# Expert weights held on chip and copied at a register's column, and spikes counted by TensorE, in a four-layer macaron kernel

## What is computed

```python
# L1 ffn: a spiking layer
h = relu(layernorm(x) @ W_fc.T) ** 2 @ W_proj.T      # 128 -> 512 -> 128
# 5 steps of a leaky integrate-and-fire neuron on input h:
#   mem = beta * mem + h - spike_before ; spike = mem > 1
# result: mean of the 5 spikes;  x = x + 0.5 * result
...
# L3 ffn, second half: a mixture of experts
ffn_probs = softmax(mean(n2, axis=1) @ ffn_rw + ffn_rb)     # one row for each sequence
topk_p, topk_i = top_k(ffn_probs, 2)
topk_p = topk_p / sum(topk_p)
h  = gelu(einsum('btd,bkdf->bktf', n2, fw1[topk_i]))        # 128 -> 256
eo = einsum('bktf,bkfd->bktd', h, fw2[topk_i])              # 256 -> 128
x  = x + einsum('bktd,bk->btd', eo, topk_p)
```

## Time and profile before

| | |
|---|---|
| median of 3 runs | 2145.94 us (2144.8 to 2148.79) |
| the profiled execution | 2153.13 us; its span, first to last instruction, 2151.4 us |
| the two spiking stages | from about 999 to 1054 us and 1224 to 1279 us of the span |
| the two expert stages | from about 1708 to 1763 us and 2083 to 2146 us |
| busy share of the span | TensorE 80%, VectorE 60%, ScalarE 54%, GpSimd 28% |

### The profile page before, as it was taken

How to read it: one execution, slowest core, us unless ns; L and a number is a source line. 1 busy time by engine, 2 the same in 40 slices (tenths; PEclk the granted TensorE clock), 3 DMA queues, 4 the chain that set the end, 5 groups by cost and what they waited for, 6 DMA issues and landing times.

```text
span 2151.4 us, 36562 instructions
## 1 busy us (share of the span) xinstructions
PE 1720.4 (80%) x13656; PEld 904.2 (42%) x13656; DVE 1294.6 (60%) x2595; ACT 1156.7 (54%) x2714; POOL 609.8 (28%) x759
## 2 busy tenths in 40 slices
PE   5896889788898879879468864986999777799976
PEld 1554345533355425543234322333555352355435
DVE  4773477444676357734667276835878445577844
ACT  3664356434465436554336545562888726388862
POOL 2551055200453025410155202303332020333202
PEclk8998999999899899989768687995999978599997
DMA  4000000000000000000063000005444020544403
GB/s 170 16 17 6 0 16 16 12 0 1 16 12 16 1 11 16 12 6 0 8 117 65 2 0 1 0 0 100 95 95 88 2 78 0 109 96 93 80 2 98
DMA packets 55270, 79.19 MB, mean 37 GB/s; under 512 B 6004, under 2 KB 38996, under 8 KB 54584
## 3 DMA queue, kind: packets, MB, share of 16 engines
q1 hardware_dynamic: 52536, 68.47, 14.5%
q0 software_dynamic: 2560, 8.39, 1.4%
HBM read 50.59 MB, written 16.88 MB: 31 GB/s over the span
## 4 chain that ended last, share of the span: by engine, by line
PE 55%; DVE 17%; ACT 14%; issue 7%; POOL 3%; DMA 3%; SPq 0%; DVEq 0%; POOLq 0%; ACTq 0%
PE ps L195 51%; ACT arena L544 4%; ACT arena L1208 2%; DVE arena L1229 2%; PE ps L463 2%; DVE arena L600 2%; ACT arena L267 2%; ACT arena L269 2%; DVE arena L643 1%; DVE arena L985 1%; DVE arena L987 1%; ACT arena L263 1%; DVE arena L983 1%; DMA arena<-scratch 1%; DVE arena L612 1%
## 5 line engine op out<-in xcount | busy, mean ns | idle before, releaser
L195 PE MATMUL ps<-arena 32*64 32x128 f32 (+10 forms) x10192 | 724.0, 319 | 129.9 <-ACT arena L1208 28.1
L195 PEld LDWEIGHTS ps<-arena 128*18 128x18 f32 (+6 forms) x10192 | 412.3, 128 | 434.8 <-issue 120.7
L1229 DVE TENSOR_REDUCE arena<-ps 128x2 f32<-128x512 f32 x512 | 322.4, 684 | 111.1 <-PE ps L195 109.1
L195 PE MATMUL ps<-arena,w_L0f 128*128 128x512 f32 (+3 forms) x800 | 352.1, 573 | 39.5 <-ACT arena L291 14.5
L1208 ACT ACTIVATE arena<-ps 128x512 f32<-128x512 f32 (+1 forms) x640 | 333.8, 576 | 78.7 <-PE ps L195 69.5
L544 ACT ACTIVATE arena<-ps,arena 128x128 f32<-128x128 f32 x512 | 226.2, 461 | 137.8 <-DVE arena L645 137.8
L195 PEld LDWEIGHTS ps<-arena,w_L0f 128*128 128x128 f32 (+2 forms) x800 | 149.4, 204 | 174.4 <-issue 127.0
L195 PE MATMUL ps<-arena,const 128*128 128x512 f32 (+1 forms) x528 | 173.1, 618 | 60.7 <-DVE arena L1657 22.3
L715 POOL TENSOR_TENSOR arena<-arena 128x512 f32<-128x512 f32 x128 | 132.2, 1040 | 239.6 <-DVE arena L617 239.6
L600 DVE TENSOR_TENSOR arena<-ps,arena 128x1024 f32<-128x1024 f32 x128 | 153.3, 1206 | 21.1 <-PE ps L195 21.1
L555 ACT ACTIVATE arena<-ps 128x512 f32<-128x512 f32 x128 | 76.8, 600 | 126.1 <-DVE arena L600 123.4
(11 more groups left out here) (223 smaller groups left out, 2150.0 us busy)
## 6 DMA issues: line engine op xcount, KB each, us to landing
scratch<-arena SPq DMA_DIRECT2D x40, 384.0 KB, 2.8
arena<-scratch SPq DMA_DIRECT2D x80, 192.0 KB
arena<-scratch SPq DMA_DIRECT2D x80, 128.0 KB
arena<-arena SPq DMA_DIRECT2D x64, 128.0 KB, 2.3
arena<-scratch SPq DMA_DIRECT2D x80, 88.0 KB
w_L0f<-in_L0f SPq DMA_DIRECT2D x2, 1557.0 KB, 12.3
arena<-arena SPq DMA_DIRECT2D x80, 12.0 KB
const<-in_const SPq DMA_DIRECT2D x1, 1276.0 KB, 7.6
```

The lines of the kernel that those rows point to most:

```text
L195: return self.nc.tensor.matmul(o, lhsT, rhs, start=start, stop=stop, skip_group_check=True)
L1229: o = V.tensor_reduce(mx, ps[:, self.score_bank(s), :].rearrange("p (t s) -> p t s", t=2), AXX, ALU.max)
```

## The change

Spiking stage. The spike of each step is written by itself, as a bf16 tile `fired[i]` of ones and zeros, with a compare of one source (lines 996, 1003); `mem` is then the plain sum of that tile and `u` (1001). `acc` is gone: TensorE adds the five tiles of a chunk, each multiplied by the bf16 unit matrix `ident_b`, in PSUM bank 6 or 7 (`count`), and VectorE adds the count to the residual (`add`, line 1014), one chunk late. There are ten `fired` tiles, for two chunks. TensorE's `count(c - 2)` stands between the up and the down products of chunk c.

Expert stage. SP loads all eight experts (8 DMAs of 256 KB) into `experts` at the stage's start. The 16 indirect DMAs are gone, and GpSimd has no work in the stage. VectorE turns each pair's expert number into a first column; for each pair it loads that number into a register (`value_load`), and copies 512 columns of `experts`, from the column in the register on, to `chosen[n]`. The first three copies are made ahead of the loop, then one in each turn, three pairs ahead. TensorE waits for `picked` in place of the DMA.

```diff
@@ Spike.tensor
             for j in range(4):
                 self.wait_ge(eng, self.relued, 4 * c + j - 3)
                 mm(ps[:, j, :], k.wp("L1f", "fcT")[:, j * P:(j + 1) * P], self.h[:, chunk(c)]).then_inc(self.up.sem, 1)
+            if c >= 2:
+                self.count(eng, c - 2)
...
+        self.count(eng, NCHUNK - 2)
+        self.count(eng, NCHUNK - 1)
+    def count(self, eng, c):
+        k = self.k
+        self.norm.wait_done(eng, 3)
+        self.wait_ge(eng, self.added, c - 1)
+        for i in range(SPIKE_STEPS):
+            self.wait_ge(eng, self.spiked, SPIKE_STEPS * c + i + 1)
+            k.mm(k.ps[:, 6 + c % 2, :], k.ident_b[:], self.fired[SPIKE_STEPS * (c % 2) + i], start=i == 0, stop=i == SPIKE_STEPS - 1).then_inc(self.counted.sem, 1)
@@ Spike.vector
-            ch.did(V.tensor_scalar(mem, y, -1.0, None, ALU.mult))
-            ch.wait_ge()
-            V.tensor_scalar(acc, mem, -1.0, None, ALU.is_lt)
-            for _ in range(SPIKE_STEPS - 1):
-                ch.did(V.scalar_tensor_tensor(u, mem, BETA, y, ALU.mult, ALU.subtract))
+            fired = self.fired[SPIKE_STEPS * (c % 2):SPIKE_STEPS * (c % 2 + 1)]
+            self.wait_ge(eng, self.counted, SPIKE_STEPS * (c - 1))
+            V.tensor_scalar(fired[0], y, 1.0, None, ALU.is_gt).then_inc(self.spiked.sem, 1)
+            ch.did(V.scalar_tensor_tensor(u, y, -BETA, y, ALU.mult, ALU.subtract))
+            for i in range(1, SPIKE_STEPS):
                 ch.wait_ge()
-                ch.did(V.scalar_tensor_tensor(mem, mem, -1.0, u, ALU.is_lt, ALU.add))
+                self.wait_ge(eng, self.spiked, SPIKE_STEPS * c + i)
+                ch.did(V.tensor_tensor(mem, fired[i - 1], u, ALU.add))
                 ch.wait_ge()
-                ch.did(V.scalar_tensor_tensor(acc, mem, -1.0, acc, ALU.is_lt, ALU.add))
-            ch.wait_ge()
-            V.scalar_tensor_tensor(k.X[:, cs], acc, 0.5 / SPIKE_STEPS, k.X[:, cs], ALU.mult, ALU.add)
+                V.tensor_scalar(fired[i], mem, -1.0, None, ALU.is_lt).then_inc(self.spiked.sem, 1)
+                if i < SPIKE_STEPS - 1:
+                    ch.did(V.scalar_tensor_tensor(u, mem, BETA, y, ALU.mult, ALU.subtract))
+            if c:
+                self.add(eng, c - 1)
+        self.add(eng, NCHUNK - 1)
+    def add(self, eng, c):
+        k, X = self.k, self.k.X[:, chunk(c)]
+        self.wait_ge(eng, self.counted, SPIKE_STEPS * (c + 1))
+        k.nc.vector.scalar_tensor_tensor(X, k.ps[:, 6 + c % 2, :], 0.5 / SPIKE_STEPS, X, ALU.mult, ALU.add).then_inc(self.added.sem, 1)
@@ L3Experts
-                eng.wait_ge(self.arrived[n].sem, self.arrived[n].at(16))
+                self.wait_ge(eng, self.picked, n + 1)
...
-        ch.did(V.tensor_scalar(self.rowf, self.rowf, k.C("partition"), None, ALU.add))
+        ch.did(V.tensor_scalar(self.rowf, self.rowf, float(EXPERT_N // P), None, ALU.mult))
         ch.wait_ge()
         V.tensor_copy(self.row_no, self.rowf).then_inc(self.rows_ready.sem, 1)
+        self.wait_ge(eng, self.arrived, 16 * EXPERTS)
+        self.wait_ge(eng, self.rows_ready, 1)
+        for n in range(AHEAD):
+            self.pick_expert(eng, n)
         for n in range(N + 2):
+            if n + AHEAD < N:
+                self.pick_expert(eng, n + AHEAD)
...
-    def gpsimd(self, eng, ch):
...
-            eng.indirect_dma_start(self.chosen[n], None, self.k.ins["experts"], bass.IndirectOffsetOnAxis(ap=rows, axis=0)).then_inc(self.arrived[n].sem, 16)
+    def pick_expert(self, eng, n):
+        i = n % TOP_K * BATCH + n // TOP_K
+        at = eng.value_load(self.row_no[0:1, i:i + 1], min_val=0, max_val=(EXPERTS - 1) * EXPERT_N)
+        self.k.nc.vector.tensor_copy(self.chosen[n], self.experts[:, bass.ds(at, EXPERT_N)]).then_inc(self.picked.sem, 1)
+    def sync(self, eng):
+        for e in range(EXPERTS):
+            eng.dma_start(self.experts[:, e * EXPERT_N:(e + 1) * EXPERT_N], self.k.ins["experts"][e * P:(e + 1) * P]).then_inc(self.arrived.sem, 16)
```

More of the change, by code:

```diff
@@ L1912, in __init__ @@
         self.chosen = [a.take(EXPERT_N) for _ in range(TOP_K * BATCH)]
+        self.experts = a.take(EXPERTS * EXPERT_N)
         self.hb = [a.take(2 * SEQ) for _ in range(3)]
```

16 lines of the change are left out of this document (7 added, 9 removed).

## The result

The changed kernel took **2120.43 us** (median of 4 runs, 2116.96 to 2127.05), the kernel before beside it 2147.36 us (4 runs): a ratio of 0.9871, 95% interval 0.9832 to 0.991, so 27 us less, and between 19 and 36. Forecast were 19.2 us and 2126.7.

| set of runs | kernel before, median us | changed kernel, median us | ratio and interval |
|---|---|---|---|
| first comparison | 2147.36 | 2120.43 | 0.9871 [0.9832, 0.991] |
| e1 to e4 | 2156.23 | 2120.38 | 0.9824 [0.9796, 0.9852] |
| e13 to e16 | 2156.75 | 2124.8 | 0.985 [0.9819, 0.988] |

A forecast was written before the change was run, and what follows sets the result against it. VectorE was taken to bound the spiking stage; the wait for indirect DMAs, then TensorE, the expert stage. Gains of 12.7 and 6.5 us off 2145.94 gave 2126.7 us, range 2120 to 2140, with 0.68 between 2121 and 2131.

The forecast's parts named there:

- VectorE's chunk, 8.12 us, and the stage, 32.7 us: Spiking stage: a chunk takes 8.12 us against 9.75, the stage 32.7 against 39.04; gain 6.3 us a stage.
- R3: Rival, spiking stage: compares into bf16 run at full price, 0.61 us for 0.35; 2137.1 us; chance 0.08.
- R4: Rival, spiking stage: only the number of instructions counts, 5.2 us gained instead of 12.7; 2134.2 us; chance 0.05.
- TensorE's counts, 1.1 us a chunk and hidden: Spiking stage: five bf16 count products take 1.1 us a chunk, delaying `y` within a cover of 0.9 us.
- The start of the expert stage, 1.23 us with x = 0.73: Expert stage: first product 1.23 us after the row numbers, against 4.48; gain 3.25 us a stage.
- x: Expert stage: time of a register load with its check and address arithmetic, taken as 0.73 us.
- The loop costs nothing: Expert loop: register loads lie beside VectorE's 1.36 us of work a pair, under TensorE's 1.73 us.
- R2: Rival, expert loop: loads stand in line at 0.73 us, costing 5.8 us a stage; 2138.4 us; chance 0.10.
- R1: Slower rival, expert loop: register loads stand in line with VectorE's work; even at 0.95 us each; chance 0.09.
- The preload, hidden: Expert stage: eight loads, 2.1 MB, take 10 us and are needed 27 us after the stage's start.
- 2145.94 - 19.2: Whole kernel: gains of 12.7 and 6.5 us taken off the median of the runs, giving 2126.7 us.
- The counts don't warm the clock: End of spiking stage: ten count products leave TensorE's clock at 0.50; otherwise the next stage saves up to 1.9 us.

The follow-up runs named there:

- e1 to e4: One set beside the kernel before: spiking change alone (ratio 0.9947), expert change alone (0.992), changed kernel again (0.9824), kernel before again (1.0014).
- e13 to e16: One set on one chip: changed kernel (2124.8 us), it with one-instruction last spiking step (2120.06), kernel before (2146.84), changed kernel with unused gathers (2156.69).
- e8: Changed kernel with the spiking stage's fired values kept in f32 and counted with the f32 identity: 2131.1 us.
- e14: Changed kernel with the last of a chunk's five spiking steps in one VectorE instruction: 2120.06 us, ratio 0.9827.
- e7: Changed kernel with every register load done twice in a row: 2128.91 us.
- e16: Changed kernel plus sixteen gathers per expert stage into unused columns, awaited by GpSimd alone: 2156.69 us in one run.
- e9: The kernel before, unchanged, profiled once more: 2146.07 us.

## Why the forecast was right in its terms and short in its sum

- **VectorE's chunk, 8.12 us, and the stage, 32.7 us:** 8.08 and 32.61. Right. The reason given for the 0.43 us of a compare, the row of the cast to bf16, and spelt out ahead of e8 as the bf16 result, was wrong (e8): it is the single source, and line 981 in rows 3 was the row to take. R3 had therefore no ground, though its price was nearly that of e8 by accident. R4 fell too: 0.34 and 0.72 us stand side by side.
- **TensorE's counts, 1.1 us a chunk and hidden:** 1.24 with the tail. Right, and e8 shows the cover used up: at 4.45 us VectorE waits 2.4 and 3 us for the last two chunks. The remaining cover is gone with 0.4 us a chunk less on VectorE (e14).
- **The start of the expert stage, 1.23 us with x = 0.73:** 1.32 us in the second stage and 1.60 in the first. Right in the main; x was chosen by nearness to GpSimd's 0.73 us, not from any load, and its closeness to the 0.8 us between cast and copy is luck.
- **"The loop costs nothing":** true in effect, with pairs at 1.73 us. The reason (the sequencer is ahead of the datapath) was half right: the load stands in line behind a waiting instruction, and runs beside the data work only after that (e7). R2's picture was nearer to the machine than its price, since it added the load to the time of the data work that it runs beside. R1's turning point, x = 0.95, lies above the 0.61 us measured.
- **The preload, hidden:** right, done 17 us before its need.
- **The step that failed is the sum:** "taken off the median: 2145.94 - 19.2". It added the two terms and put everything else in the kernel at nothing: TensorE's clock (at the expert stage's start in so many words, "I count nothing for that") and whatever the going of 32 indirect DMAs may give beside the wait. Against the kernel before the changed kernel gained 27 us, and 25.6 us (1.8) over all its runs, against those of before on chips without the stall. About 20 us of that are in the four stages, as forecast: 12.8 for 12.7 in the spiking stages, 7.3 for 6.5 in the expert stages. The other 5 us lie outside the terms. They go with a granted clock that is higher than the cut of the slow stretches explains, 0.909 for about 0.904; what raises it stays open. The gathers' going isn't shown to be it: with unused gathers added, runs without gaps average 2124.1 us for 2122.0, no difference clear of the noise.
- **The kernel before was taken as steady.** On two of the six sets' chips its gathers cost it some 9 us more (2156 against 2147 us), by the gaps that e16 ties to them. In the first comparison the stall isn't the answer, as before took 2147 us there. The shown profile of before had no stall, so no row of it priced that.
- **The counts don't warm the clock:** right. The stage behind the first spiking stage starts at a granted clock of 0.50 (1045.88 to 1048.88 us), and its first products take 3.78 us, as before. The range reached down to 2120 us by a warm clock there and a load near 0.03 us, and neither came; what brought the time to that edge was in no term.

## What to carry to other kernels

Sum VectorE's work by start-to-start spacings and by form: one source in SBUF 0.34 us, or 0.46 where the next waits, two sources 0.72, for 512 columns; that gave a 6.4 us change to 0.1 us. A selection made at run time from a small table is cheaper as a resident copy, a register load (0.6 us in line) and an on-chip copy (0.43) than as an indirect DMA (4.5 us to the first product), as long as the table's own load is hidden and the register load fits beside the engine's work: one a pick did, two did not. And profile the kernel before more than once, on more than one chip, before taking a difference off its median: here it moved by 9 us from chip to chip, a third of the gain. Compare the mean granted clock of the two kernels as well; here it stood for 5 to 6 us that no stage accounts for.

## What the runs showed of the hardware that was not expected

- On two chips, sixteen indirect DMAs of 256 KB each held back TensorE's signals from about the sixth product of the stage, even with no other engine waiting for them (e16). The longest step between two Gelus was 5.0 to 7.9 us, the expert stages grew by 3.5 to 11 us, and the signals all came within 0.3 us of the end of the last gather's packets. The packets themselves were on time (20 to 21 us in all).
- A register load from SBUF with its bounds check and address arithmetic takes VectorE's sequencer 0.61 us, the load alone 0.30; it starts only when the waiting instruction ahead of it is let go.
- TensorE's clock in the L1 attention stage: 0.74 over the stage in the shown profile of before (168.6 us), 0.84 in e9 (156.4 us), with the same instructions.
